# Attention in groups of four tiles: value products, casts, projection and scaling in two PSUM banks in turn

## What is computed

```python
scores = jnp.einsum('bhqd,bhkd->bhqk', q, k) * SCALE
kb = -p * jnp.log1p(a * dist)
attn = jax.nn.softmax(scores + kb[None], axis=-1)
out = jnp.einsum('bhqk,bhkd->bhqd', attn, v)
out = out.transpose(0, 2, 1, 3).reshape(Bb, Ss, H * D)
return out @ out_w.T
```

## Time and profile before

| | us |
|---|---|
| median of 3 runs | 1763.08 (1762.02 to 1769.2) |
| the profiled execution, its own time | 1762.21 |
| its span | 1760.5 |
| PE busy | 1621.9 (92%) |
| DVE busy | 1496.0 (85%) |
| POOL busy | 1413.8 (80%) |
| ACT busy | 1177.6 (67%) |
| `bias_max` (L1153), 512 times | 620.3, 1.220 each |
| low parts (L1271), 512 times | 953.7, 1.895 each |
| exponentials (L1235), 512 times | 588.2, 1.149 each |

### The profile page before, as it was taken

How to read it: one execution, slowest core, us unless ns; L and a number is a source line. 1 busy time by engine, 2 the same in 40 slices (tenths; PEclk the granted TensorE clock), 3 DMA queues, 4 the chain that set the end, 5 groups by cost and what they waited for, 6 DMA issues and landing times. The chain is left out here.

```text
span 1760.5 us, 39216 instructions
## 1 busy us (share of the span) xinstructions
PE 1621.9 (92%) x12064; PEld 890.5 (51%) x12064; DVE 1496.0 (85%) x3046; ACT 1177.6 (67%) x1806; POOL 1413.8 (80%) x820
## 2 busy tenths in 40 slices
PE   4879989858999999999999999999999999689998
PEld 3435655423555555555555555555555555346666
DVE  7778978996888989898898989888898989567876
ACT  6536544537877878777877877787787877644441
POOL 5676847857999999999999999999999999553554
PEclk9899999988999999999999999999999999889999
DMA  5466856768989889889889989989989988500110
GB/s 161 136 182 191 225 157 184 197 201 189 177 193 218 186 180 233 181 184 228 181 190 213 194 176 221 194 183 210 198 189 199 210 179 171 120 18 1 31 31 25
DMA packets 735171, 296.46 MB, mean 168 GB/s; under 512 B 630192, under 2 KB 697778, under 8 KB 735104
## 3 DMA queue, kind: packets, MB, share of 16 engines
q1 hardware_dynamic: 732304, 292.17, 73.9%
q0 software_dynamic: 2048, 3.15, 0.9%
q10 hardware_dynamic: 768, 0.53, 0.1%
HBM read 101.34 MB, written 58.85 MB: 91 GB/s over the span
## 5 line engine op out<-in xcount | busy, mean ns | idle before, releaser
L1271 POOL TENSOR_TENSOR probs_lo<-probs 128x1024 bf16<-128x1024 f32 x512 | 953.7, 1895 | 80.5 <-ACT probs L1235 79.9
L1235 ACT ACTIVATE probs<-scores,neg_max 128x1024 f32<-128x1024 f32 x512 | 588.2, 1149 | 220.1 <-DVE neg_max L1153 211.4
L1153 DVE CUSTOM_DVE_ANT_0 scores<-score_ps,bias_tab 128x1024 f32<-128x1024 f32 x512 | 620.3, 1220 | 76.9 <-issue 69.8
L1067 PE MATMUL score_ps<-x 128*128 128x512 bf16 x1024 | 308.5, 383 | 31.5 <-PEq L294 17.8
L1083 PEld LDWEIGHTS turn_ps<-ident_bf,probs 128*128 128x128 bf16 x4096 | 261.1, 98 | 146.0 <-issue 55.9
L1083 PE MATMUL turn_ps<-ident_bf,probs 128*128 128x128 bf16 x4096 | 313.9, 219 | 0.2
L1102 PE MATMUL pv_ps<-probs_t_hi,v_hi_lo 128*128 128x512 bf16 x1024 | 263.6, 380 | 0.3 <-DVE share L1185 0.3
L1242 ACT COPY probs_t_hi<-turn_ps 128x1024 bf16<-128x1024 bf16 x256 | 253.8, 991 | 0.0
L439 POOL TENSOR_TENSOR qk_parts<-rotated,qk_parts 128x1024 bf16<-128x1024 f32 x64 | 137.4, 2152 | 84.0 <-ACT qk_parts L872 83.6
L1168 DVE COPY probs_t_hi<-turn_ps 128x1024 bf16<-128x1024 bf16 x256 | 172.6, 674 | 0.8 <-PE turn_ps L1083 0.8
L1589 POOL TENSOR_TENSOR q_state<-state,q_t 128x1024 f32<-128x1024 f32 x32 | 76.0, 2375 | 107.2 <-PE s_ps L1766 71.3
(11 more groups left out here) (236 smaller groups left out, 2311.1 us busy)
## 6 DMA issues: line engine op xcount, KB each, us to landing
x<-qk_parts SPq DMA_DIRECT2D x192, 256.0 KB, 3.4
qk_parts<-qk_parts SPq DMA_DIRECT2D x252, 128.0 KB, 2.5
v_hi_lo<-v_parts SPq DMA_DIRECT2D x64, 256.0 KB, 3.0
bias_tab<-bias_by_distance SPq DMA_DIRECT2D x64, 240.0 KB, 3.8
v_parts<-bias_tab SPq DMA_DIRECT2D x52, 256.0 KB, 2.9
probs_t_lo<-probs_lo SPq DMA_TRANSPOSE x512, 3.2
v_stacked<-v_three SPq DMA_DIRECT2D x72, 32.0 KB, 1.9
g<-in_x SPq DMA_DIRECT2D x4, 512.0 KB, 6.3
```

The costliest lines, as they stand in the source:

```text
L1067: pe.matmul(sp_[n % 2][:, cs], QB[s][:, q], KK[s][:, cs], start=True, stop=False)
L1153: v.tensor_tensor_reduce(SB[n % 2][:], sp_[n % 2][:], TB[s][:, j:j + S], -SCALE, 3.0e38, ALU.add, ALU.min, neg_max[:, n % 16:n % 16 + 1]). ...
L1235: act.activation(PR[n % NP][:], SB[n % 2][:], ACT.Exp, bias=neg_max[:, m:m + 1], scale=-1.0, accum_out=row_sum[:, m:m + 1]).then_inc(exped, 1)
L1271: g.tensor_tensor(LQ[n % NL][:], PR[n % NP][:], PRB[n % NP], ALU.subtract).then_inc(low_made, 1)
```

## The change

- Value products, casts, projection and scaling go by groups `g` of four tiles (Q = 4): group `g` uses bank `g` mod 2, and each group goes through all of its steps by itself. In its four steps PE does four high products, one, three and the first pair of low parts, and three pairs of low parts.
- The two products of a pair of low parts now belong to one group: even key blocks go to the lower 64 partitions of its bank, odd ones to the upper 64 of the same bank.
- The cast of both banks is ACT's (`take_out`), four steps behind the group's first; both low parts stay DVE's (`out_low`), one in a group. The projection (`out`) comes one step later, 12 products, after `turn` and ahead of the value products of that step.
- `LV` is 3 for 2, and scores, exponentials and transposes run 8, 7 and 5 tiles ahead of `n`, where it was 12, 11 and 9.
- In DVE's step `bias_max` comes first, then `out_low` (`n` mod 4 = 0), `scale_share` (`n` mod 8 = 6), `add_share` (2), `invert` (2) and the copy.
- The waits on `pv_ready` count groups; `load_v` waits for `pv_ready` at tiles 0 and 8 of an iteration where it waited for `op_ready` at 2 and 10. `pv_ready`, `ot_hi` and `ot_ready` are single semaphores.

The diff follows, empty lines left out; of `by_v` and `out` only the new lines are shown (the old ones are L1086 to L1122).

```diff
@@ -933,7 +933,7 @@
     s_ready, biased, exped = sem("s_ready"), sem("biased"), sem("exped")
     turned, hi_act, hi_dve = sem("turned"), sem("hi_by_act"), sem("hi_by_dve")
     low_made, lo_in = sem("low_made"), [sem(f"lo_in{i}") for i in range(4)]
-    pv_ready, ot_ready, op_ready = sem("pv_ready"), [sem(f"ot_ready{c}") for c in range(2)], sem("op_ready")
+    pv_ready, ot_hi, ot_ready, op_ready = sem("pv_ready"), sem("ot_hi"), sem("ot_ready"), sem("op_ready")
     scaled, added, add_begun = sem("scaled"), sem("added"), sem("add_begun")
     recip = sem("recip")
@@ -949,7 +949,6 @@
     OH = [sb(f"out_t_hi{i}", [P, CH], BF16) for i in range(2)]
     OL = [sb(f"out_t_lo{i}", [P, CH], BF16) for i in range(2)]
     SH = sb("share", [P, 4, D])
-    ot_hi = [sem(f"ot_hi{c}") for c in range(2)]
     neg_max, row_sum = sb("neg_max", [P, 16]), sb("row_sum", [P, 16])
     inv = sb("inv_sum", [P, 16])
     gate = sb("wait_holder", [P, 2])
@@ -971,9 +970,11 @@
     NI = B * G
     U = 2 * BT
-    LV = 2
-    LS, LE, LT = LV + 12, LV + 11, LV + 9
-    HI_STEPS, V_STEPS, OUT_STEP, PROJ_STEP = 4, 6, 6, 7
+    Q = 4
+    LV = 3
+    LS, LE, LT = LV + 8, LV + 7, LV + 5
+    HIGH, LOW = [range(0, 4), range(4, 5), range(5, 8), ()], [(), (), range(0, 1), range(1, 4)]
+    TAKE, PROJ, SCALE_AT = Q, Q + 1, Q + 2
     def run(eng, step):
@@ -1009,7 +1010,7 @@
                 r = n % U
                 sp.wait_ge(low_made, at(it, U, n + 1))
                 if n % BT == 0 and not (isinstance(it, int) and it == 0):
-                    sp.wait_ge(pv_ready, at(it, 2, n // BT - 1))
+                    sp.wait_ge(pv_ready, at(it, 4, 2 * (n // BT) - 2))
                 sp.sem_inc(add_begun, 1)
                 sp.dma_start(LO[:, r, :, :], LQ[n % NL][:], transpose=True).then_inc(lo_in[n % NL], DMA)
@@ -1018,8 +1019,8 @@
                 for n in range(U):
                     lo_turn(it, n)
                     s = n // BT
-                    if n % BT == 2 and not (isinstance(it, int) and it == 0):
-                        sp.wait_ge(op_ready, at(it, 4, 2 * (s + 1) - 4))
+                    if n % BT == 0 and not (isinstance(it, int) and it == 0):
+                        sp.wait_ge(pv_ready, at(it, 4, 2 * (s + 1) - 4))
                         load_v(it, s)
                     if n in LOADS and not (last and b == B - 1):
                         s = LOADS.index(n)
@@ -1083,43 +1084,39 @@
...
                     mm = pe.transpose(tp[n % 2][:, k, :], PRB[n % NP][:, k * P:k * P + P], ident16[:])
                 mm.then_inc(turned, 1)
+            def by_v(it, g, j):
+
+                h, i = g // 2 % 2, g % 2
+                r = BT * h + Q * i
                 if j == 0:
+                    if i == 0:
+                        pe.wait_ge(v_in[h], at(it, DMA, DMA * (g // 4 + 1)))
+                    copied(pe, it, Q * g + Q - 2)
+                    copied(pe, it, Q * g + Q - 1)
+                    pe.wait_ge(scaled, at(it, 4, g + 1))
+                for k in HIGH[j]:
+                    pe.matmul(ov[i][:], VV[h][:, k, :], PT[:, r:r + Q, k, :], start=(k == 0), stop=False, skip_group_check=True)
+                if LOW[j] and 0 in LOW[j]:
+                    for l in range(NL):
+                        pe.wait_ge(lo_in[l], at(it, DMA * U // NL, DMA * Q // NL * (g + 1)))
+                for pair in LOW[j]:
+                    for c in range(2):
+                        k = 2 * pair + c
+                        mm = pe.matmul(ov[i][c * DH:c * DH + DH], VV[h][:, k, 0:DH], LO[:, r:r + Q, k, :],
+                                       start=False, stop=(pair == BT // 2 - 1), skip_group_check=True)
+                if j == Q - 1:
                     mm.then_inc(pv_ready, 1)
+            def out(it, g):
+                i, w = g % 2, it // B * 2 + g // 2
+                w_hi, w_lo = [WB[:, a, bass.ds(w, 1), :].rearrange("p o m -> p (o m)") for a in range(2)]
+                pe.wait_ge(ot_ready, at(it, 4, g + 1))
+                for k in range(Q):
+                    q = slice(k * P, k * P + P)
+                    pe.matmul(ov[i][:, k, :], OH[i][:, q], w_hi, start=(k == 0), stop=False, skip_group_check=True)
+                    pe.matmul(ov[i][:, k, :], OH[i][:, q], w_lo, start=False, stop=False, skip_group_check=True)
+                    mm = pe.matmul(ov[i][:, k, :], OL[i][:, q], w_hi, start=False, stop=True, skip_group_check=True)
+                mm.then_inc(op_ready, 1)
             def step(it, u, there):
                 n = u + LV
@@ -1131,10 +1128,10 @@
                 if pair:
                     scores(it, u + LS + 1)
                     high_parts(u + LS)
-                if there(n) and n % BT == PROJ_STEP:
-                    out(it, n // BT)
-                if there(n) and n % BT < V_STEPS:
-                    by_v(it, n // BT, n % BT)
+                if there(n - PROJ) and (n - PROJ) % Q == 0:
+                    out(it, (n - PROJ) // Q)
+                if there(n):
+                    by_v(it, n // Q, n % Q)
             run(pe, step)
@@ -1163,18 +1160,15 @@
             def untile(it, n):
                 if n % BT == 1 and not (isinstance(it, int) and it == 0 and n < U):
-                    v.wait_ge(pv_ready, at(it, 2, n // BT - 1))
+                    v.wait_ge(pv_ready, at(it, 4, 2 * (n // BT) - 2))
                 v.wait_ge(turned, at(it, U, n + 1))
                 v.tensor_copy(PT[:, n % U, :, :], tp[n % 2][:]).then_inc(hi_dve, 1)
-            def take_out(it, hh):
-
-                v.wait_ge(pv_ready, at(it, 2, hh + 1))
-                v.tensor_copy(OH[1][:], ov[1][:].rearrange("p t q -> p (t q)")).then_inc(ot_hi[1], 1)
-                for c in range(2):
-                    v.wait_ge(ot_hi[c], at(it, 2, hh + 1))
-                    v.tensor_tensor(OL[c][:], ov[c][:].rearrange("p t q -> p (t q)"), OH[c][:],
-                                    ALU.subtract).then_inc(ot_ready[c], 1)
+            def out_low(it, g):
+
+                i = g % 2
+                v.wait_ge(ot_hi, at(it, 4, g + 1))
+                v.tensor_tensor(OL[i][:], ov[i][:].rearrange("p t q -> p (t q)"), OH[i][:], ALU.subtract).then_inc(ot_ready, 1)
             def scale_share(it, hh):
@@ -1198,17 +1192,16 @@
             def step(it, u, there):
                 n = u + LV
-                hh, j = n // BT, n % BT
-                if there(n) and j == OUT_STEP:
-                    take_out(it, hh)
                 if there(u + LS):
                     bias_max(it, u + LS)
-                if there(n - BT) and j == 1:
-                    add_share(it, hh - 1)
-                if there(n) and j == 2:
-                    invert(it, hh)
-                if there(n) and j == PROJ_STEP:
-                    scale_share(it, hh)
+                if there(n - TAKE) and (n - TAKE) % Q == 0:
+                    out_low(it, (n - TAKE) // Q)
+                if there(n - SCALE_AT) and (n - SCALE_AT) % BT == 0:
+                    scale_share(it, (n - SCALE_AT) // BT)
+                if there(n - SCALE_AT) and (n - SCALE_AT) % BT == Q:
+                    add_share(it, (n - SCALE_AT) // BT)
+                if there(n) and n % BT == 2:
+                    invert(it, n // BT)
                 if there(u + LT) and by_dve(u + LT):
                     untile(it, u + LT)
@@ -1237,21 +1230,22 @@
             def untile(it, n):
                 if n % BT == 0 and not (isinstance(it, int) and it == 0 and n < U):
-                    act.wait_ge(pv_ready, at(it, 2, n // BT - 1))
+                    act.wait_ge(pv_ready, at(it, 4, 2 * (n // BT) - 2))
                 act.wait_ge(turned, at(it, U, n + 1))
                 act.copy(PT[:, n % U, :, :], tp[n % 2][:]).then_inc(hi_act, 1)
-            def take_out(it, hh):
-
-                act.wait_ge(pv_ready, at(it, 2, hh + 1))
-                act.copy(OH[0][:], ov[0][:].rearrange("p t q -> p (t q)")).then_inc(ot_hi[0], 1)
+            def take_out(it, g):
+
+                i = g % 2
+                act.wait_ge(pv_ready, at(it, 4, g + 1))
+                act.copy(OH[i][:], ov[i][:].rearrange("p t q -> p (t q)")).then_inc(ot_hi, 1)
             def step(it, u, there):
                 n = u + LV
-                if there(n) and n % BT == OUT_STEP:
-                    take_out(it, n // BT)
                 if there(u + LE):
                     exp(it, u + LE)
+                if there(n - TAKE) and (n - TAKE) % Q == 0:
+                    take_out(it, (n - TAKE) // Q)
                 if there(u + LT) and not by_dve(u + LT):
                     untile(it, u + LT)
                 if isinstance(it, int) and it == NI - 1 and u + LT == U + 1:
@@ -1281,7 +1275,7 @@
             def step(it, u, there):
                 if there(u + LT):
                     low(it, u + LT)
-                if there(u) and u % BT == BT - 1:
+                if there(u - 4) and u % BT == 4:
                     add_share(it, u // BT)
             g.nop().then_inc(added, 1)
```

(20 more changed lines are left out.)

## The result

The changed kernel takes 1900.35 us against 1764.01 for the kernel before, measured beside it. (1900.35 is the median of four runs: three lie between 1899.13 and 1900.81, and the fourth, of 2834.75 with a mean granted clock of 0.69, is left out of the ratio.) The ratio is 1.0753, with a 95% interval from 1.0732 to 1.0775; the two medians alone give 1.077. The forecast was 1852 with a range up to 1885: slower, as forecast, but by 7.5% and not by 5.0%.

A forecast was written before the change was run, and what follows sets the result against it. PE was taken to bound the kernel before, with DVE's loop close behind; after the change DVE's loop decides. 1762.2 + 92 (score pairs at 4.66 us) - 2 (end) = 1852 us, +5.0%, range 1815 to 1885.

The forecast's parts named there:

- The bound and the loop: PE bounds the kernel before, DVE's loop close behind; after the change that loop decides, 18.63 us a half against 17.18.
- 3.41 + X: Time from O to O in us; X is DVE work between E and O, forecast at 1.21 to 1.30.
- ACT's cast: ACT takes the second cast, 0.574 us, in time for `out_low` by 0.4: no cost; rival of being late: 1890, chance 0.04.
- the shared bank: Both column halves of low parts in one bank cost nothing; rival that they take turns: 1925, chance 0.05.
- The borders: On PE, borders of tiled shapes, 16 for 11 a half: +0.55 us, lying under DVE's loop.
- The projection's tie in steps 0 and 4: PE's path from `out_low` through the projection and DVE's loop both reach the O products at 5.91; 0.03 us added per pair.
- O: The odd tile of a pair; its `bias_max` start marks the loop, counted from O to O.
- E: The even tile of a pair; its `bias_max` takes 1.14 us in the loop.
- DVE's burst of 4.70: Kernel before, steps 5 and 6: a copy, a cast and two subtractions between O and E make the loop 4.70 us.
- Edges: Fill and end of the stage: 4 pairs at 4.02 for 6; value work behind the last scores shorter, -2 us.
- the bound of 0.1 us a pair: The forecast's own uncertainty on the pair time, either way: 25 us, 1827 to 1877.
- the rival that expected a gain from moving the second cast to ACT (1751): PE's work decides, not the order on DVE: -11 us, 1751, chance 0.06.

## Why the prediction was right and wrong

- **The bound and the loop**: right. 3.41 + X was read from the fill of the stage, and pairs without other delays take 4.61 and 4.62 for 4.62. Moving DVE's extras out of X gave back the whole loss. The granted clock stayed at 1.00 in the stage, and ACT's cast, the shorter lead of the low parts and the shared bank cost nothing that the rows show.
- **The borders**, +0.55 us under cover: right (one block for two, no change).
- **The projection's tie in steps 0 and 4**: half right. Where the address is ready it costs nothing (4.61 and 4.62), so the 0.03 added was too much. In every second group the address is worked out once the wait is over (PE begins 0.16 behind `out_low` for 0.05, its second product another 0.07 late), and the path through PE then is the longer one: 0.20 and 0.23. With fixed weights 0.40 an iteration went.
- **The term that failed is the size of the steady loop**, 18.63 for 19.33 a half. I summed instructions with a duration and took idle time on DVE in the critical place as nought. Four things stand there that have no busy row: the back edge (0.41 an iteration), the table wait's value (0.30), the weights' address on PE (0.43) and the 0.16 left open; and the reciprocal, in the sum with 0.12, held DVE 0.24, which cost 0.11 twice with the gap ahead of it. Together, with the rounding of the pairs, 1.51 an iteration, less 0.12 by which I had rounded up the tie; 1.39 x 31 iterations = 43 us.
- **These delays were there before, and smaller.** In the kernel before, the back edge lay between an O and an E, in the free gap, and the projection with its address came ahead of the O products that waited for DVE's burst of 4.70 anyway. They were not free there: every second half is 0.43 us longer (17.40 from O at 834.74 to O at 852.14, and 16.97 from 817.77 to 834.74), in two places. Its rows are

```profile
838.76 1.22 DVE L1153 CUSTOM_DVE_ANT_0 scores<-score_ps,bias_tab 128x1024 f32<-128x1024 f32 x1
...
841.28 1.23 DVE L1153 CUSTOM_DVE_ANT_0 scores<-score_ps,bias_tab 128x1024 f32<-128x1024 f32 x1
...
843.11 1.22 DVE L1153 CUSTOM_DVE_ANT_0 scores<-score_ps,bias_tab 128x1024 f32<-128x1024 f32 x1
...
845.67 1.22 DVE L1153 CUSTOM_DVE_ANT_0 scores<-score_ps,bias_tab 128x1024 f32<-128x1024 f32 x1
```

  where O to E takes 2.52 directly over the back edge (2.37 in the other half) and 2.56 at the wait for the bias table (2.31 in the other half). So about 0.4 us an iteration was already in the 17.18, and a comparison of its two halves would have shown these delays before the forecast. I checked the moved operations against X and not the moved back edge: `LV` went from 2 to 3, and I had costed that at nothing.
- **Edges**: the remainder behind the last O was +0.6 for -2. The stage began 3.6 us later; the first `bias_max` of the ten kernels spreads over 7.1 us, so this is no effect of the change that these rows could show. The 43 us of the loop, 3.6 and 2.6 make 49.2, against 48.6 between 1852.2 and the profiled 1900.81.
- **POOL's work** was put too high, at no price. 16.44 adds durations that overlap by a little; its busy time from 600 to 1400 us in the kernel before is 749.6 of 800, which is 16.1 a half.
- **Range**: the bound of 0.1 us a pair had no row behind it but the fit in the fill, where the steps have no address and no back edge (they are written out). The unpriced waits averaged 0.17 a pair and put the result 15 us above the range. The kernel before had 0.69 us of waiting in a half besides PE's work, and I gave the new loop none; that remainder as the upper bound (0.69 x 63 = 43 us on top) would have reached 1895, still short of 1900.
- **The pages drawn on.** The Trainium skill (PSUM — Partial Sum Buffer, section "PSUM bank collisions raise a hardware error") quotes that different column tiles can access one bank at the same time: the trace agrees, 0.22 us a pair in one bank as in two. The Trainium skill (TensorEngine Tiling, section "PSUM Bottleneck") advises to use both ScalarE and VectorE for emptying PSUM. Both kernels do; the rival that expected a gain from moving the second cast to ACT (1751) fell, since DVE's busy time was not what bound.

## What to carry to other kernels

In a software pipeline with two buffers look for the loop through two engines, and price a moved operation by whether it lands on it: here 0.6 us of DVE work cost all of its length between E and O, and nothing behind O. Measure that loop where the pipeline fills, since there nothing else covers it, but add from the steady stage what the fill does not have: the loop's back edge, waits on values worked out from the loop's index, dynamic addresses. When a pipeline's offset is changed, find out where its back edge falls.

## What the runs showed of the hardware that I had not expected

- A back edge of a hardware loop held DVE 0.41 us where nothing covered it (0.40 an iteration by the experiment), a wait on a value with a division in it about 0.30 us, and a dynamic weight address on PE about 0.2 us. The Trainium skill (Advanced Engine Details and Errata, Control Flow Timing) gives a compare-and-branch about 0.11 us; the whole edge measured here is nearly four times that.
- Behind a stand of 1.87 or 1.91 us in each half TensorE's clock fell to 1.2 GHz in 40 of 49 halves (mean 0.60 over 4.3 us in one of them) and stayed at 2.4 GHz in nine, which put 1.34 us a half on top of a wait that cost 1.47. With stands of up to 0.6 us, in the changed kernel, it did not fall. What decides between the 40 and the nine is not shown here.
- The profile's label for a wait can name an instruction that has nothing to do with it. Behind both "<-ACT probs" stood the waiting engine's own register and loop work: all of the 0.40 at 852.00, and 0.26 of the 1.29 at 825.54, of which 1.03 is the ordinary wait for PE (as at 835.03).
